# A fused four-layer graph network on one core: the GAT input loaded twice, the adjacency in four loads, P squared's copies moved, and new lists of steps

## The chip, the cores and the metric

The kernel runs on one core of a Trainium2 chip. Its time is the device time of one execution, in microseconds (us). Before the change the median of three runs was 1242.79 us (1241.85 to 1243.12).

## The reference

The input x has B = 16 batches of N = 512 nodes with D = 128 features, float32; adj is one 512 x 512 adjacency matrix for all batches. Four layers follow one another, each as x = x + layer(relu(layernorm(x))):

```python
# layer 0: eight Euler steps of a diffusion
h = h @ fc_in_w.T + fc_in_b
w_eff = w * clip(d, 0, 1) @ w.T
for _ in range(8):
    f = sigmoid(alpha)[:, None] * 0.5 * (adj @ h - h) + h @ w_eff - h + x0
    h = h + f / 8
# layer 1, GAT: attention over the graph
Wh = h @ W
e = leaky_relu(Wh @ a1 + (Wh @ a2).T); e = where(adj == 0, -inf, e)
out = softmax(e) @ Wh
# layer 2, edge: attention over 256 edges src -> dst, softmax by source node, then @ W_out.T
# layer 3: Chebyshev propagation, attention with 4 heads, feed-forward
L_norm = 2 * adj / (eigvalsh(adj)[-1] + 1e-8) - I
x1 = relu(layernorm((L_norm @ x) @ Wc + bc)) + x
x2 = layernorm(x1 + attention(x1 @ Wq, x1 @ Wk, x1 @ Wv, mask=adj > 0) @ Wo + bo)
out = layernorm(x2 + gelu(x2 @ W1 + b1) @ W2 + b2)
```

## The kernel before, in words

**Two programs behind one another.** `build_front` (line 563) computes what all batches share, the whole of layer 0, and, beside the last quarter of layer 0, layers 1 and 2 of the first batch and the start of layer 1 of the second. It ends near 453 us. `build_layers` (line 1824) does the rest as a pipeline over batches. Each engine runs its own program; they meet at semaphores. The engines are TensorE (PE), VectorE (DVE), ScalarE (ACT), GpSimd (POOL) and SyncE (SP), which issues the loads and stores, one behind another.

**Layer 0.** The eight Euler steps are written as polynomials: P = (sigmoid(alpha)/16) (adj - I), R = w_eff/8 + (7/8) I. The kernel loads adj in one transfer (line 683), transposes it on PE (`turn_adj`, line 1327) for S and the later Laplacian, transposes the 128 x 128 tiles of the weights (`turn_weights`), then those of P (`turn_p`, line 1341), keeps PT as a high and a low part of reduced precision (`keep_p`, `p_low`), and multiplies P by itself (`p_product`, line 1349). PE then makes R's powers (`r_product`), the products of R's powers with the fc weights and bias (`fc_products`, line 1369, and `bias_products`, line 1375). P squared is read out of PSUM by ACT, which writes its high part (P2T_hi, line 914), and by DVE (`p_squared`, line 1043), which writes a plain copy and the low part. In ACT's order the four copies of P2T_hi stand behind the ReLUs of batches 0 to 3; in DVE's, `r_powers(2)` stands behind `p_squared(0)` and `p_squared(1)`.

The 16 batches go through in four chunks of four. Batch by batch PE transposes the normalised input (`turn_x0`, line 1391) and applies P and P squared to it (`apply_p`, line 1398); the input z is split into a high part (ACT, `split_z`) and a low part (DVE, `split_z`, line 960); the products come out as U1 (kept by ACT) and U2 (kept by DVE, `keep_u2`, line 965). In chunk 0 each batch also makes a quarter of P cubed. Then per chunk three levels of four tiles follow (`right_products`, `p3_times`), which multiply with G, the polynomial table in R that DVE builds during chunk 0 (`polynomial`, line 1108).

**Asides and slots.** The largest eigenvalue of adj comes from nine squarings of a matrix S, hidden beside layer 0. Each batch and each tile is a *slot*, numbered through from 0; `aside(slot)` puts a piece of the squaring there, five slots to one squaring: the square sum (ACT), the norm's sum over partitions (PE, into PSUM), its reciprocal `nrm` (DVE, line 993), the scaled copies (ACT). In DVE's loop over batches (lines 1277 to 1296) the order is: split z of the batch after next, keep U2, cube and polynomial in chunk 0, and the aside last. On PE a transposition of the next batch's input (`turn_x0`) writes the same PSUM bank as the norm's sum, so it waits for `nrm`.

**Masks.** POOL makes two masks from adj in one instruction each: mask_gat (line 769), ahead of the first chunk's work, and mask_att (line 784), behind the square sums, in chunk 3.

**The pipeline.** Each stage of a batch (gat, edge, cheb, att, ffn) is cut into steps with a function each. `run` (line 1952) gives each engine its steps by lists written out by hand: FILL_ORDER (step:batch), then a loop whose iteration i runs each step of ORDER for batch i minus the stage's lag (gat 0, edge 1, cheb 2, att 3, ffn 4; each "+" behind a name is one batch more), then DRAIN_ORDER. The loop is rolled and runs iterations FILL to 15; FILL = 5 here, so 11 iterations. In the trace fill spans 453 to 579 us, the loop 579 to 1100, the drain the rest.

**GAT.** `load_x` (line 408) loads batch n's layer 0 output (256 KB) into xA once the last reader of xA for the batch before is done. `gat_stats` (line 456) reads xA, `gat_apply` (line 466) writes the normalised value to zA, `gat_turn` transposes zA on PE, ACT applies the ReLU (`gat_hT`, line 430), `gat_wh` is the first product. `gat_x2` (line 500), the stage's end, adds xA as the residual.

**Chebyshev, attention, ffn.** `cheb_prop` (line 2363 in the trace) multiplies by the Laplacian; its input is split by ACT (`cheb_hi`) and DVE (`cheb_lo`, line 2163). Q and K of each head go through memory and are loaded *stacked*, high and low part together (`stack0` to `stack3`). The attention runs 16 tiles: score (PE, line 2356), mask (DVE, line 2198), exponential (ACT, line 2100), turn (PE, line 2410), copy (ACT, line 2109), and at the end the product with V. In ffn the GELU's first call loads a table (ACT_TABLE_LOAD). An engine's copy from PSUM for several stages goes through one helper line, as L2085 on ACT.

## Time and profile before

| What | Value |
| --- | --- |
| Median of three runs | 1242.79 us (1241.85 to 1243.12) |
| The profiled execution | 1239.62 us, its span 1237.8 us |
| Granted TensorE clock, mean | 0.98 of full speed |
| PE busy | 1127.5 us (91%), 7537 instructions |
| DVE busy | 836.7 us (68%), 3039 instructions |
| ACT busy | 759.9 us (61%), 1625 instructions |
| POOL busy | 346.4 us (28%), 481 instructions |
| DMA | 83.59 MB moved, mean 68 GB/s |

The profile is of one execution of 1239.62 us; its times count from its own start, and the span ends 1.8 us short of that execution's time. A clock of 1.0 is 2.4 GHz and 0.5 is 1.2 GHz. An engine's busy time adds up its instructions; waits at semaphores, branches and the issue of DMAs are not in it. The columns of the rows are told at each group.

### The profile page before, as it was taken

The page shows a single profiled execution, that of the slowest core. Times are in us where ns is not written, and L with a number is a line of the kernel's source. Part 1 is how long each engine was busy: PE and PEld are TensorE (multiplying, and loading weights), DVE is VectorE, ACT ScalarE, POOL GpSimd, SP SyncE. Part 2 cuts the span into 40 slices and gives each one's busy share as a digit, 9 for nine tenths or more (in the row PEclk, how much of TensorE's full clock was granted, in tenths as well). Part 3 has the DMA queues.
Part 4 walks back from the last instruction along what each step waited for, and adds up shares of the span by engine and source line. Part 5 has one row for each costly group of instructions (what it writes and reads, how often), then busy time and mean ns, then how long its engine had stood idle before and what let it go on. Part 6 is the DMA issues. An engine that isn't in the chain of part 4 may idle for free. (4 is left out here: it accounts for less than half of the span.)

```text
span 1237.8 us, 23622 instructions
## 1 busy us (share of the span) xinstructions
PE 1127.5 (91%) x7537; PEld 894.1 (72%) x7537; DVE 836.7 (68%) x3039; ACT 759.9 (61%) x1625; POOL 346.4 (28%) x481
## 2 busy tenths in 40 slices
PE   7889999999999978899899999999999999999775
PEld 4568879889879865677767677677677677676554
DVE  5544213214336547888988988889889889888666
ACT  4314224333213235887978878878878878888763
POOL 3204006004042122242343333333423422422122
PEclk9899999999999989999999999999999999999898
DMA  5011020020010002334243242242242341342430
GB/s 126 17 33 28 26 73 5 27 76 2 26 52 1 27 26 67 88 86 105 58 119 88 65 119 76 72 123 62 82 120 61 90 119 51 102 109 68 109 91 26
DMA packets 123819, 83.59 MB, mean 68 GB/s; under 512 B 13296, under 2 KB 106864, under 8 KB 123760
## 3 DMA queue, kind: packets, MB, share of 16 engines
q1 hardware_dynamic: 123696, 82.82, 24.9%
q8 instruction: 34, 0.56, 0.2%
q14 instruction: 25, 0.20, 0.1%
q0 software_dynamic: 64, 0.00, 0.0%
HBM read 28.25 MB, written 20.97 MB: 40 GB/s over the span
## 5 line engine op out<-in xcount | busy, mean ns | idle before, releaser
L2100 ACT ACTIVATE att_Es<-att_Ts,att_small 128x512 f32<-128x512 f32 x256 | 184.8, 722 | 61.3 <-DVE att_small L2198 60.8
L2198 DVE CUSTOM_DVE_ANT_0 att_Ts<-bank,mask_att 128x512 f32<-128x512 f32 x256 | 174.2, 682 | 33.1 <-PE bank L2356 30.6
L2410 PE MATMUL bank<-ident,att_Es 128*128 128x128 f32 x1024 | 159.7, 279 | 20.1 <-ACT att_PTs L2109 18.8
L2410 PEld LDWEIGHTS bank<-ident,att_Es 128*128 128x128 f32 x1024 | 120.9, 142 | 62.4 <-ACT att_PTs L2109 35.6
L2109 ACT COPY att_PTs<-bank 128x512 f32<-128x512 f32 x248 | 143.4, 578 | 34.4 <-PE bank L2410 33.3
L2356 PE MATMUL bank<-K_parts,Q_parts 128*128 128x512 f32 x256 | 125.1, 498 | 2.7 <-DMA K_parts<-k_lo 1.8
L1908 POOL TENSOR_SCALAR n_rs<-n_mv 128x4 f32<-128x4 f32 x46 | 14.0, 304 | 289.0 <-DVE n_mv L1903 289.0
L424 POOL TENSOR_SCALAR gat_Vs<-gat_Ts,gat_small 128x512 f32<-128x512 f32 x64 | 57.7, 916 | 81.5 <-DVE gat_small L490 81.4
L974 DVE TENSOR_TENSOR P_row<-bank,l_bias 128x512 f32<-128x512 f32 x32 | 22.1, 691 | 84.0 <-PE bank L1426 65.9
L1416 PE MATMUL bank<-G,x0T 128*128 128x128 f32 x384 | 74.8, 276 | 0.7 <-DVE U2T L967 0.5
L1416 PE MATMUL bank<-G,U1T 128*128 128x128 f32 x384 | 74.3, 275 | 0.0
L1416 PE MATMUL bank<-G,U2T 128*128 128x128 f32 x384 | 74.2, 275 | 0.0
L722 POOL TENSOR_SCALAR l_rs<-l_mv 128x4 f32<-128x4 f32 x16 | 6.8, 425 | 230.9 <-DVE l_mv L958 230.6
L551 PE MATMUL bank<-gat_whs,gat_ETs 128*128 128x128 f32 x512 | 64.4, 282 | 2.1 <-PEq L141 2.0
L1416 PEld LDWEIGHTS bank<-G,x0T 128*128 128x128 f32 x384 | 60.5, 191 | 4.3 <-issue 1.7
L551 PEld LDWEIGHTS bank<-gat_whs,gat_ETs 128*128 128x128 f32 x512 | 61.2, 196 | 3.0 <-issue 2.5
L2356 PEld LDWEIGHTS bank<-K_parts,Q_parts 128*128 128x128 f32 x256 | 48.3, 194 | 20.6 <-issue 16.2
L1416 PEld LDWEIGHTS bank<-G,U2T 128*128 128x128 f32 x384 | 58.3, 192 | 0.0
L1416 PEld LDWEIGHTS bank<-G,U1T 128*128 128x128 f32 x384 | 58.3, 192 | 0.0
L442 ACT ACTIVATE gat_Ts<-gat_Vs,gat_small 128x512 f32<-128x512 f32 x64 | 46.3, 724 | 17.1 <-DVE gat_Vs L494 17.1
L2478 PE MATMUL bank<-att_PTs,v_in 128*32 128x512 f32 x480 | 54.3, 592 | 0.0
L1426 PE MATMUL bank<-Z_hi,P3T_hi 128*128 128x512 f32 x128 | 52.9, 414 | 0.0
(330 smaller groups left out, 2930.8 us busy)
## 6 DMA issues: line engine op xcount, KB each, us to landing
Q_parts<-q_hi SPq DMA_DIRECT2D x128, 64.0 KB, 2.0
Q_parts<-q_lo SPq DMA_DIRECT2D x128, 64.0 KB, 2.0
K_parts<-k_hi SPq DMA_DIRECT2D x128, 64.0 KB, 2.0
K_parts<-k_lo SPq DMA_DIRECT2D x128, 64.0 KB, 2.0
l_x<-in_x SPq DMA_DIRECT2D x16, 256.0 KB, 2.9
P2T<-in_x SPq DMA_DIRECT2D x16, 256.0 KB, 4.6
x_after_l<-P2T SPq DMA_DIRECT2D x16, 256.0 KB, 2.3
gat_xin<-x_after_l SPq DMA_DIRECT2D x16, 256.0 KB, 4.0
```

What stands on the lines that cost most here:

```text
L424: nc.gpsimd.tensor_scalar(g.V[:, t, :], g.T[:, t, :], 0.2, small[:, 5, t:t + 1], ALU.mult, ALU.add).then_inc(sem("gat_low"), 1)
L442: nc.scalar.activation(g.T[:, t, :], g.V[:, t, :], ACT.Exp, bias=small[:, 4, t:t + 1], accum_out=small[:, 6, t:t + 1]).then_inc(sem("gat_e ...
L551: mm = nc.tensor.matmul(a0[:, cols(t)], g.ET[:, s, cols(t)], WhA[:, s, 0:D], start=(s == 0), stop=(s == NT - 1))
L974: nc.vector.tensor_tensor(by_batch(zs[:, t, :]), by_batch(bank[t][:]), bias[:, BLOCKS - 1 - lev, t:t + 1, :].broadcast_to([P, CB, D]), ALU.add
L1416: mm = nc.tensor.matmul(bank[t][:, b * D:(b + 1) * D], UT[i][:, b, cols(t)], G[:, STEPS - k0 - i, :], start=(b == 0 and i == 0), stop=(lev ...
L1426: mm = nc.tensor.matmul(bank[t][:], left[:, s, cols(t)], right[:, s, :], start=False, stop=(s == NT - 1 and i == 2))
L2100: nc.scalar.activation(att_E[:, j % RING_E, :], att_T[:, j % RING_T, :], ACT.Exp, scale=-1.0, bias=att_small[:, 0, j:j + 1], accum_out=att ...
L2109: nc.scalar.copy(att_PT[:, h, :, cols(q)], c2[:].rearrange("p (s q) -> p s q", q=P)).then_inc(sem("att_pt"), 1)
L2198: nc.vector.tensor_tensor_reduce(att_T[:, j % RING_T, :], [c0, c1][j % 2][:], k.mask_att[:, tile_of(n, j)[1], :], -QK_SCALE, HUGE, ALU.add ...
L2356: return nc.tensor.matmul(dst, left, right, start=True, stop=True)
L2410: mm = nc.tensor.transpose(dst[:, cols(s)], att_E[:, i % RING_E, cols(s)], k.ident[:])
L2478: mm = nc.tensor.matmul(b0[r, :], vD[:, s, r], att_PT[:, h, s, :], start=(s == 0), stop=(s == NT - 1))
```

## The change

1. The GAT input is loaded twice: `load_z` fills zA for the statistics and the normalising, which is now done in place; `load_x` fills xA, read only by the residual addition at the stage's end. `load_z` waits for PE's transposes of the batch before, `load_x` for the last residual addition as before.
2. In the front, adj comes in four loads of 128 rows, each with its own semaphore (shared with the later loads of the residual). PE transposes the rows' tiles in the order in which they are loaded, then P (`turn_p`), then the weights. DVE makes P's rows as they come. The four semaphores stand for the one in POOL too.
3. ACT copies the high part of P squared (`square_hi`) right behind P's: two copies ahead of the first ReLU, two behind the second; the casts of S and the other ReLUs follow. DVE's order is p_squared(0), r_powers(0), the row sums of P, p_squared(1), r_powers(1), statistics(2), p_squared(2), statistics(3), r_powers(2), p_squared(3), then the splits of z.
4. In DVE's loop over batches the aside comes first from chunk 1 on, and in chunk 0 right behind U2 and the split of z, ahead of the cube and the polynomial; keeping U2 comes ahead of the split of z.
5. POOL makes mask_att in four instructions, and behind `edge_pick` instead of ahead of it.
6. ORDER, FILL_ORDER and DRAIN_ORDER are written anew. In ORDER six steps gain a "+": load_x3, ffn_final, store_out, stack0 and stack2, edge_store, so FILL becomes 6: the loop runs 10 iterations, and one more batch is written out in FILL_ORDER. On PE gat_turn moves from behind cheb_g to ahead of ffn_wo, gat_wh in between cheb_prop1 and cheb_g, and some turns, scores and ffn products change places. On DVE ffn_final+ and att_rv+ move to the top, the GAT statistics ahead of the masks. On ACT gat_hT moves up between att_exp1 and att_exp2, att_copy2 behind ffn_x2T, att_copy3 between the two GELUs.

```diff
@@ gat_stage
     def on_sync(sp):
+        def load_z(n):
+            wait_alone(sp, sem("gat_turned"), n, sem("waits_passed"))
+            sp.dma_start(zA[:], k.nodes1(k.x1_dram, n)).then_inc(sem("gat_zloaded"), 16)
         def load_x(n):
             wait_alone(sp, sem("gat_done"), n * NT, sem("waits_passed"))
...
         def gat_stats(n):
-            ready(dve, "gat_loaded", n, 16, 16)
+            ready(dve, "gat_zloaded", n, 16, 16)
             for t in range(NT):
-                nc.vector.bn_stats(g.stat[:, t, :], xA[:, t, :]).then_inc(sem("gat_stat"), 1)
+                nc.vector.bn_stats(g.stat[:, t, :], zA[:, t, :]).then_inc(sem("gat_stat"), 1)
...
         def gat_apply(n):
+            ready(dve, "gat_stat", n, NT, NT)
             ready(dve, "gat_rs", n)
             for t in range(NT):
-                nc.vector.tensor_scalar(zA[:, t, :], xA[:, t, :], ...
+                nc.vector.tensor_scalar(zA[:, t, :], zA[:, t, :], ...
...
         def gat_x2(n, t0):
             if t0 == 0:
+                ready(dve, "gat_loaded", n, 16, 16)
                 ready(dve, "gat_rinv", n)
@@ build_front, SP
-            load(adj[:], t_in["adj"].rearrange("(t p) m -> p t m", p=P), "adj_loaded")
+            for t in range(NT):
+                load(adj[:, t, :], t_in["adj"][t * P:(t + 1) * P, :], f"rows_loaded{t}")
@@ build_front, POOL
-            pool.wait_ge(sem("norm_part"), SQUARINGS)
-            nc.gpsimd.tensor_scalar(k.mask_att[:], adj[:], 0.0, MASKED / QK_SCALE, ALU.is_le, ALU.mult
-                                    ).then_inc(sem("masks"), 1)
             pool.wait_ge(sem("u_ready"), 2 * B)
             for t in range(NT):
                 nc.gpsimd.tensor_scalar(k.edge_pick[:, t, E:], edge_f[:, 1, :], node_col[:, t:t + 1], None,
                                         ALU.is_equal).then_inc(sem("pick"), 1)
+            pool.wait_ge(sem("norm_part"), SQUARINGS)
+            for t in range(NT):
+                nc.gpsimd.tensor_scalar(k.mask_att[:, t, :], adj[:, t, :], 0.0, MASKED / QK_SCALE, ALU.is_le, ALU.mult
+                                        ).then_inc(sem("masks"), 1)
@@ build_front, ACT
+            def square_hi(s):
+                act.wait_ge(sem("p_square"), s + 1)
+                nc.scalar.copy(P2T_hi[:, s, :], bank[4 + s][:]).then_inc(sem("P2T_hi"), 1)
+
+            square_hi(0)
+            square_hi(1)
             for b in range(2):
                 relu(b)
                 split_z(b)
+            square_hi(2)
+            square_hi(3)
             act.wait_ge(sem("asym"), NT)
             nc.scalar.copy(S[0][:], asym[:]).then_inc(sem("scaled"), 1)
             for b in range(2, CB):
                 relu(b)
-            for s in range(NT):
-                act.wait_ge(sem("p_square"), s + 1)
-                nc.scalar.copy(P2T_hi[:, s, :], bank[4 + s][:]).then_inc(sem("P2T_hi"), 1)
@@ build_front, DVE
+            p_squared(0)
+            r_powers(0)
             nc.vector.tensor_reduce(pone[:, 0, :], P_row[:], AX, ALU.add).then_inc(sem("p_one"), 1)
-            r_powers(0)
-            for b in range(2, CB):
-                statistics(b)
+            p_squared(1)
             r_powers(1)
-            for s in range(2):
-                p_squared(s)
+            statistics(2)
+            p_squared(2)
+            statistics(3)
             r_powers(2)
+            p_squared(3)
             for b in range(2):
                 split_z(b)
-            for s in range(2, NT):
-                p_squared(s)
...
                     b = ch * CB + j
+                    if ch:
+                        aside(slot)
+                    keep_u2(b)
                     if j < CB - 2:
                         split_z(b + 2)
-                    keep_u2(b)
                     if ch == 0:
+                        aside(slot)
                         p_cubed(j)
...
-                    aside(slot)
                     slot += 1
@@ build_front, PE
+            def turn_adj():
+                for t in range(NT):
+                    pe.wait_ge(sem(f"rows_loaded{t}"), 16)
+                    for s in range(NT):
                         mm = nc.tensor.transpose(bank[4 + s][:, cols(t)], adj[:, t, cols(s)], k.ident[:])
+                        if t == NT - 1:
+                            mm.then_inc(sem("adj_turned"), 1)
...
-            turn_adj("adj_turned", None)
+            turn_adj()
+            turn_p()
             turn_weights()
-            turn_p()
@@ ORDER
     "PE": """
-        att_score0 att_score1 att_turn15+ att_rows+ att_pv0+ att_pv1+ att_score2 att_turn0 att_score3 cheb_prop0
-        ffn_wo att_turn1 att_score4 cheb_prop1 cheb_g gat_turn att_turn2 att_score5 gat_wh ffn_turn att_turn3 gat_s2
-        ffn_up0 att_score6 ffn_up1 att_turn4 ffn_down0 att_score7 ffn_down1 att_turn5 att_score8 cheb_x1turn att_turn6
...
+        att_score0 att_score1 att_turn15+ att_rows+ att_pv0+ att_pv1+ att_score2 att_turn0 att_score3 gat_turn ffn_wo
+        cheb_prop0 att_turn1 att_score4 cheb_prop1 gat_wh cheb_g att_turn2 ffn_turn att_score5 gat_s2 ffn_up0
+        att_turn3 att_score6 ffn_up1 att_turn4 att_score7 ffn_down0 ffn_down1 att_turn5 att_score8 cheb_x1turn
...
     "DVE": """
-        cheb_stats cheb_aggr gat_x2a+ gat_x2b+ edge_stats att_mask0 edge_aggr att_mask1 cheb_lo gat_stats gat_aggr
-        att_mask2 att_scale att_mask3 gat_apply ffn_y2 n2_stats att_mask4 n2_aggr cheb_y n2_apply n1_stats att_mask5
...
+        cheb_stats ffn_final+ cheb_aggr gat_x2a+ gat_x2b+ att_rv+ gat_stats gat_aggr att_mask0 edge_stats edge_aggr
+        att_mask1 gat_apply cheb_lo att_scale att_mask2 att_mask3 ffn_y2 n2_stats n2_aggr att_mask4 n2_apply cheb_y
...
     "ACT": """
-        cheb_apply cheb_hi att_spread+ att_exp0 att_exp1 att_exp2 att_copy0 att_exp3 edge_apply cheb_xpT att_copy1
-        att_exp4 gat_hT att_copy2 edge_hi gat_wh_out0 gat_wh_out1 ffn_x2T att_exp5 att_copy3 ffn_gelu0 ffn_gelu1
-        att_exp6 att_copy4 att_exp7 att_copy5 cheb_x1T att_exp8 att_copy6 gat_exp0 edge_hg gat_exp1 edge_xz att_exp9
...
+        cheb_apply cheb_hi att_spread+ att_exp0 att_exp1 gat_hT att_exp2 att_copy0 att_exp3 edge_apply cheb_xpT
+        att_copy1 gat_wh_out0 att_exp4 edge_hi gat_wh_out1 ffn_x2T att_copy2 att_exp5 ffn_gelu0 att_copy3 ffn_gelu1
+        att_exp6 att_copy4 att_exp7 att_copy5 cheb_x1T att_exp8 att_copy6 gat_exp0 edge_hg gat_exp1 edge_xz
...
     "POOL": """
-        cheb_rstd edge_rstd ffn_res gat_rstd n2_rstd n1_rstd ffn_b2 edge_lo gat_low0 gat_low1 gat_low2 gat_low3
+        cheb_rstd gat_rstd edge_rstd ffn_res n2_rstd ffn_b2 edge_lo n1_rstd gat_low0 gat_low1 gat_low2 gat_low3
...
     "SP": """
-        load_xr load_x3 load_x stack1+ stack3+ store_v+ load_v cheb_res stack0 stack2 edge_store store_out
+        load_z load_x3+ stack0+ stack2+ store_out+ load_xr stack1+ load_x stack3+ edge_store+ store_v+ load_v cheb_res
...
@@ FILL_ORDER, its beginning
     "PE": """
-        gat_pv0:1 gat_pv1:1 cheb_prop0:0 cheb_prop1:0 cheb_g:0 edge_gather0:1 edge_gather1:1 gat_turn:2 edge_x:1
+        gat_pv0:1 gat_pv1:1 cheb_prop0:0 cheb_prop1:0 cheb_g:0 gat_turn:2 gat_wh:2 gat_s2:2 edge_gather0:1
...
     "DVE": """
-        cheb_stats:0 gat_rinv:1 cheb_aggr:0 gat_x2a:1 gat_x2b:1 edge_stats:1 edge_aggr:1 cheb_lo:0 gat_stats:2
+        cheb_stats:0 cheb_aggr:0 gat_rinv:1 gat_x2a:1 cheb_lo:0 gat_x2b:1 gat_stats:2 gat_aggr:2 edge_stats:1
...
```

## Rows read from the trace of the kernel before

**Rows 1.** Busy by stage: stretch, length, busy (count) of PE, PEld, DVE, ACT, POOL, clock, DMA.

```profile
14.25:44.04 29.79, 24.46 (x81) 12.93 (x81) 20.52 (x69) 12.14 (x24) 18.84 (x21) 0.89 0.17 31
450.00:484.89 34.89, 24.17 (x130) 19.05 (x130) 23.61 (x94) 12.89 (x29) 10.48 (x17) 0.90 0.14 40
484.89:628.22 143.33, 131.98 (x923) 101.87 (x923) 119.87 (x468) 116.00 (x264) 43.25 (x66) 0.99 0.32 85
628.22:1099.99 471.77, 441.04 (x3223) 338.69 (x3222) 419.76 (x1631) 395.81 (x880) 165.49 (x231) 1.00 0.33 89
1099.99:1237.80 137.81, 107.96 (x785) 75.51 (x783) 97.21 (x339) 91.06 (x195) 31.55 (x44) 0.92 0.31 82
```

**Rows 2.** Timeline (start, duration, engine, line, operation, tiles, shape, [idle before]): SP's load of adj.

```profile
1.24 0.50 SPq L674 DMA_DIRECT2D adj<-in_adj  x1
```

**Rows 3.** Timeline of PE: transposes of adj and P, first product with P.

```profile
6.81 3.67 PE L1332 MATMUL bank<-ident,adj 128*128 128x128 f32 x16 [6.81 <-DMA adj<-in_adj]
...
11.07 1.91 PE L1346 MATMUL bank<-ident,P_row 128*128 128x128 f32 x16
...
14.25 3.70 PE L1352 MATMUL bank<-PT,P_row 128*128 128x512 f32 x8 [1.26 <-DVE PT L1035]
```

**Rows 4.** Timeline, 33 to 44 us: the mask, P squared's copies, fc and bias products.

```profile
33.26 7.12 POOL L769 TENSOR_SCALAR mask_gat<-adj 128x2048 bf16<-128x2048 f32 x1
...
35.36 0.69 DVE L1045 COPY P2T<-bank 128x512 f32<-128x512 f32 x1 [9.00 <-ACT P2T_hi L914]
...
38.49 3.46 PE L1372 MATMUL bank<-Rp,raw_fcw 128*128 128x512 f32 x4 [5.04 <-DVE Rp L1067]
...
42.25 1.96 PE L1379 MATMUL bank<-Rp,fcb_b 128*128 128x512 f32 x4 [0.29 <-DVE pone L1273]
```

**Rows 5.** Timeline: G's operations, the transposes behind the reciprocal at slot 1 and later.

```profile
65.08 3.23 DVE L1114 SCALAR_TENSOR_TENSOR G<-Rp,G 128x128 f32<-128x128 f32 x15
...
68.45 0.81 PE L1395 MATMUL bank<-ident,l_x 128*128 128x128 f32 x4 [4.52 <-DVE nrm L993]
...
251.42 0.66 PE L1395 MATMUL bank<-ident,l_x 128*128 128x128 f32 x4 [0.74 <-DVE nrm L993]
```

**Rows 6.** Busy by stretch, columns as in rows 1: behind three waits.

```profile
68.45:76.00 7.55, 7.55 (x28) 6.20 (x29) 0.00 (x0) 1.84 (x3) 0.00 (x0) 0.77 0.14 37
164.26:171.84 7.58, 7.58 (x28) 6.27 (x29) 0.00 (x0) 1.84 (x3) 0.00 (x0) 0.77 0.12 35
362.37:366.79 4.42, 4.42 (x12) 3.49 (x13) 1.87 (x9) 0.00 (x0) 1.39 (x1) 0.62 0.01 2
```

**Rows 7.** Timeline of PE: the transposes behind the reciprocal at slot 17.

```profile
164.26 1.05 PE L1395 MATMUL bank<-ident,l_x 128*128 128x128 f32 x4 [2.05 <-DVE nrm L993]
```

**Rows 8.** Timeline: a split of z in chunk 0, then chunk 3 with the mask.

```profile
61.13 0.69 DVE L962 TENSOR_TENSOR z_split<-l_x,z_split 128x512 fp32r<-128x512 f32 x1 [1.85 <-ACT z_split L813]
...
356.66 7.10 POOL L784 TENSOR_SCALAR mask_att<-adj 128x2048 bf16<-128x2048 f32 x1
357.21 4.50 DVE L962 TENSOR_TENSOR z_split<-l_x,z_split 128x512 fp32r<-128x512 f32 x1 [6.24 <-ACT z_split L813]
...
362.37 0.79 PE L1407 MATMUL bank<-P2T_hi,z_split 128*128 128x512 f32 x1 [2.55 <-DVE U2T L967]
```

**Rows 9.** Waits, 628.22 to 1099.99 us: us in total, times, longest us.

```profile
DVE gat_stat L459 <- DMA gat_xin<-x_after_l: 13.0, 10, 1.7
...
PE bank L2501 <- ACT ffn_mT L2093: 11.0, 10, 1.1
...
PE bank L2352 <- ACT cheb_xTs L2085: 6.9, 10, 0.7
PE bank L2352 <- DVE att_oTs L2277: 6.1, 10, 1.1
```

**Rows 10.** Timeline of ACT: a table load ahead of GELU in the loop.

```profile
835.25 1.28 ACT L2093 ACT_TABLE_LOAD   x1
```

**Rows 11.** Timeline of PE: the first propagation, in the fill.

```profile
461.82 0.79 PE L2363 MATMUL bank<-lap_hi,h_hi 128*128 128x512 f32 x1 [3.19 <-DVE h_lo L2163]
```

310 lines of the change are left out of this document (165 added, 145 removed).

## The prediction

> **What bounds the kernel now.** I read the busy time by stage first [rows 1]; the columns to compare are the length of a stretch and the matmul engine's (PE's) busy time in it. From 628 to 1100 us, ten batches at 47.2 us, PE is busy 441.04 of 471.77 us, so it sets the pace and 3.07 us a batch are its waits. VectorE (DVE) follows with 419.76 us. So a gain must come out of PE's idle time or out of stretches where its clock was granted at half. Idle are 5.3 us between the first product with P and 44.04, 10.7 and 11.4 us while the pipeline fills, 30.7 us in the loop and 29.9 us at the end. Next I went through PE's timeline for each idle stretch and what ended it, and through the waits of the loop.
>
> **Start: adjacency in four loads, P turned ahead of the weights.** One load is issued at 1.24 us [rows 2] and ends PE's first wait at 6.81; 16 transposes take 3.67 us; P's own turning starts at 11.07 and the first product with P at 14.25, after 1.26 us of waiting for DVE's copy [rows 3]. With quarters the transposes of three are done by the time the fourth lands. It carries the same last byte, so I leave it at 6.8; its four transposes take 0.9 us (a quarter of 3.67), until 7.7 instead of 10.5. ScalarE (ACT) can then no longer copy between transposes: its four copies, some 0.55 us each, end at 10.0, and P's turning ends behind them, at 10.5 to 11.6 by the clock. DVE's last copy of P follows, so the first product starts near 12.3: **1.95 us saved**. Ends: 3 us if PE runs at full speed by then, 0.5 us if the three added issues of 0.50 us [rows 2] push the last landing. The weights' five transposes fall into PE's wait and cost nothing; without that cover they are 0.6 us.
>
> **P squared's copies.** PE stood 5.04 us until 38.49 because DVE's copy of the highest power of R is queued behind P squared's first halves, and these waited 9.00 us for ACT [rows 4], whose copies stood behind four batches' ReLUs. The two fc products then ran at half clock, 3.46 us against 1.96 us for the next pair of the same shape, and the bias products waited 0.29 us more. In the new lists each copy follows its product. Without a stall the stretch is: 19.2 us from the first product to 33.45 (38.49 less 5.04), then 1.96 and 1.96, together 23.1 of the present 29.79 us: **6.7 us saved**. I followed the other queues through it with the old durations: DVE has R's power at 28.7 (PE wants it at 31.5), ACT has the cast of S at 29.6 and the fourth ReLU at 33 (PE wants its result 12 us later), GpSimd (POOL) ends its sums for batch 3 at 31.2.
>
> **The norm's reciprocal ahead of other work.** At slot 1 PE has made the norm's sum and waits 4.52 us for its reciprocal, since DVE first runs 15 operations of G, 3.23 us [rows 5]. The same hand-over with nothing ahead costs 0.74 us (at 251.42). Moving the reciprocal first leaves 0.74: 3.8 us. The idle spell was followed by half clock: 7.55 us at a mean of 0.77 [rows 6] lose 1.7 us. **5.5 us saved.** At slot 17 it is 2.05 us [rows 7] with 7.58 us at 0.77: 1.3 and 1.7, **3.0 us saved**. What waits behind the reciprocal now is U2's copy and G: U2 is read one slot, some 6 us, later, and G is done near 80 of the present clock, ten us before its reader; that slack is their cover.
>
> **POOL's big mask.** In chunk 3 DVE's split of z took 4.50 us instead of 0.69 while POOL made the attention mask in one instruction of 7.10 us begun 0.55 us before it; U2 came late and PE waited 2.55 us [rows 8], then ran 4.42 us at 0.62 [rows 6], 1.7 us lost. The mask now stands behind the edge tables, in four pieces. **4.2 us saved.** It falls beside layer 0's additions of the last chunk, where DVE's subtractions have two SBUF inputs again; a piece may hold one by up to 1.8 us, but the first matmul that reads them comes 2 to 4 us later, so I count zero (ends 0 and 2). The Trainium skill's page "SBUF — State Buffer", section "Who interferes with whom", says that a VectorE instruction with two SBUF inputs and a GpSimd one that reads SBUF exclude each other for a whole instruction, whichever starts first. The trace agrees here (4.50 us against 0.69).
>
> Layer 0 with the start: 21.4 us.
>
> **The input loaded twice.** In the loop DVE waits 1.3 us a batch for that load [rows 9], since it may start only when the previous batch's last reader is done. The second buffer is free after PE's transposes, half a batch earlier. The wait goes, but DVE is not the bound; its worth is that normalising, transposing and the GAT's first product can come earlier, into PE's holes. The 16 added loads of 256 KB go onto SP's queue, at most 0.50 us of issue each [rows 2]. The first stands behind one wait that is long over, and the stacked Q and K of heads 1 and 3 move ahead of the other; the tightest, head 1's, keeps the margin of 0.7 us it has. They are hidden.
>
> **New lists in the loop.** PE waits there 1.10, 0.69 and 0.61 us a batch for GELU, the Chebyshev copy and the scaled output [rows 9]. The new list puts GAT's product between the second propagation and its reader, GAT's transposes ahead of the output product, and a score ahead of the down product. The first two waits so covered go (1.3 us). Against that the copy behind attention turn 3 now stands behind the first GELU and the 1.28 us table load [rows 10]: exponential 0.8, table 1.28, GELU 0.64, copy 0.5, together 3.2 us, against 2.4 us of PE work; turn 5 waits similarly for the table coming back. Walking one batch through the new lists with the old durations I get some 2.3 us of waits instead of 3.07: 0.75 us a batch, for the 11 batches from the third on **8.2 us**. Ends: 0 and all three waits, 2.4 us a batch.
>
> **Fill and drain.** The first propagation waited 3.19 us for DVE's low part [rows 11], ahead of which stood GAT's last additions and edge's statistics; all but the first pair of these additions now stand behind it, 2.4 us of work by my walk. With the half clock after the wait and shorter waits later I take **4 us** of the 22 idle (ends 0 and 8). At the end, **1.8 us** of 29.9 (ends minus 2 and 6).
>
> **Sum.** 21.4 + 8.2 + 4 + 1.8 = 35.4 us. The profiled execution took 1239.62 us; 1204.2 after. The median of the runs is 3.2 us above that execution, so 1207.4 us.
>
> **Rivals.**
> 1. *A new lock at the start.* POOL's other big mask now starts at 31.3 by my walk, DVE's second split of z at 30.75. If POOL is first, DVE stands as in [rows 8], some 4.4 us from POOL's start, until 35.7; the bias products then start at 36.6 instead of 33.2 and PE's clock halves after the wait: 5.1 us given back, 1212.5 us. For it: half a microsecond of margin in a walk whose steps are good to 0.3. Against: the mask took 7.12 us from 33.26 in the old kernel [rows 4] and nobody stood, since DVE's work came after its first 4.4 us. By the skill's rule on that page the outcome hangs on who starts first, which is this rival.
> 2. *The lists only move the waits.* ACT's table load and, at the top of the loop, POOL's residual addition beside DVE's low part (my walk puts them 0.2 us apart) take back what was won: loop and drain 0, fill 2. 1239.62 − 23.4 + 3.2 = 1219.4 us.
> 3. *Slower: GAT's early transposes hold ACT.* GAT's ReLU now stands ahead of the third exponential. If its input comes late, all exponentials wait. It decides from 0.5 us late on (that is the slack of the first copy behind it); at 3.5 us late each of 14 batches loses 3 us and gains 0.75: 31.5 us lost against 21.4 won, with nothing from fill and drain, 1252.9 us. Against: its load is issued some 20 us ahead.
> 4. *Quarters do not land earlier.* The last lands 1.5 us later than the whole did; then only 0.5 us of the first term stays, 1208.9 us. The skill's "DMA: Bandwidth & Descriptors", section "Bandwidth", asks for 1 MiB or more per DMA, which speaks for this rival; no row here shows a quarter of this load.
>
> **How the numbers follow.** Forecast 0.60, rival 1 0.17, rival 2 0.16, rival 3 0.03, rival 4 0.04. Low end: 1.5 instead of 0.75 us a batch, 8 us more, and 1 us of the first term: 1198. High end: rival 2, and half of rival 1's price with it: 1222. A measurement of this kernel can tell 0.2% (2.5 us) from no change. Only rival 3 is above: slower 0.03; 0.01 for a mixture near zero; faster 0.96.
>
> **What would show it.** Right: the first product with P near 12.3; P transposes of batch 0 near 35.5 us with no wait over 1 us before; 0.7 us at both reciprocals; no split of z over 0.7 us in chunk 3; the clock at full from 15 us to the end of layer 0; layer 0's last product some 21 us earlier; no DVE wait for GAT's input; a batch in the loop at 46.4 us, PE's waits at GELU and the copy behind turn 3. Wrong: a split of z of 3 to 5 us beside the first mask (rival 1); 47.2 us a batch (rival 2); ACT idle before GAT's ReLU by more than 1 us (rival 3); PE's last adjacency transposes after 9 us (rival 4).

## The result, and the profile after

The changed kernel took 1206.66 us in the median of four runs (1199.74 to 1207.36) where the kernel before took 1242.32 us (1241.63 to 1243.12): a ratio of 0.9697, 95% interval 0.9658 to 0.9736. Six more runs on another chip gave 1206.33 us (1200.88 to 1208.19) against 1246.19 us, ratio 0.9672 (0.9639 to 0.9705). The forecast was 1207.4 us, range 1198 to 1222.

The four runs spread over 8 us where the four of the kernel before lay within 1.5, but on the other chip eleven runs of the kernel before spread over 12 us (1240.31 to 1252.38) and six of the changed one over 7, so a wide spread did not come with the change. The profiled execution is one of the short ones, 1199.74 us with a span of 1197.9 us. A second profile, of an execution of 1205.45 us, is read beside it below. So the time fell by 40.0 us between the first two profiles (1237.84 to 1197.86) and by 34.2 us to the second. The sum of the prediction, 35.4 us, is to be held against both.

The busy time by stage answers to [rows 1]. Columns as there: stretch, its length, busy time and count of PE, PEld, DVE, ACT and POOL, granted clock, DMA share and GB/s. The cuts are at 12.3 and 37 us in the front, at layer 0's last product, at the first scores of batches 0, 3 and 13, and at the end.

```profile
12.30:37.00 24.70, 24.70 (x94) 14.35 (x93) 23.02 (x68) 12.39 (x25) 17.86 (x21) 1.00 0.31 58
421.08:460.57 39.49, 27.67 (x160) 20.08 (x159) 26.78 (x102) 17.65 (x41) 11.22 (x19) 1.00 0.21 57
460.57:600.97 140.40, 128.25 (x916) 101.24 (x915) 119.88 (x465) 112.94 (x260) 43.74 (x66) 0.99 0.34 90
600.97:1056.39 455.42, 433.59 (x3223) 338.62 (x3222) 416.43 (x1631) 393.07 (x880) 165.63 (x231) 1.00 0.36 97
1056.39:1197.86 141.47, 110.45 (x785) 75.80 (x783) 96.49 (x340) 90.50 (x195) 31.53 (x44) 0.91 0.31 83
```

In the front's stretch PE has no idle time left and its full clock in this execution. Ten batches of the loop take 455.42 us instead of 471.77, 45.5 us each; the same 3223 matmuls are busy for 433.59 us instead of 441.04. The end, with the same 785 matmuls, is longer: 141.47 against 137.81 us.

Where PE reached the same points, in the three profiles (start times of the first transposes, products or scores, from the timelines):

| PE's point | Before | After, 1st | After, 2nd | Saved, 1st | Forecast |
| --- | --- | --- | --- | --- | --- |
| first product with P | 14.25 | 11.85 | 12.05 | 2.40 | 1.95 |
| x0 transposes, batch 0 | 44.04 | 34.43 | 36.33 | + 7.21 | 6.7 |
| x0 transposes, batch 3 | 80.36 | 64.89 | 66.79 | + 5.86 | 5.5 |
| x0 transposes, batch 8 | 251.42 | 232.53 | 234.43 | + 3.42 | 3.0 |
| layer 0's last product | 444.43 | 421.08 | 426.19 | + 4.46 | 4.2 |
| first score, batch 2 | 579.44 | 553.61 | 560.23 | + 2.48 | 4 |
| first score, batch 13 | 1099.99 | 1056.39 | 1063.00 | + 17.77 | 8.2 |
| end of the span | 1237.84 | 1197.86 | 1203.66 | - 3.62 | 1.8 |

**Start.** DVE makes P's rows as the quarters land. Its timeline, and PE's:

```profile
4.24 0.49 DVE L1029 TENSOR_SCALAR P_row<-adj,sg 128x512 f32<-128x512 f32 x1 [0.43 <-DMA adj<-in_adj]
...
6.88 0.49 DVE L1029 TENSOR_SCALAR P_row<-adj,sg 128x512 f32<-128x512 f32 x1 [0.24 <-DMA adj<-in_adj]
...
8.60 1.98 PE L1365 MATMUL bank<-ident,P_row 128*128 128x128 f32 x16 [0.31 <-DVE P_row L1034]
```

The last quarter is there at 6.88 us, where the whole was at 6.81 [rows 3]. The loads share the same last byte, as assumed. The first quarter is there at 4.24.

**P squared and the reciprocals.** PE's timeline of the front has no wait over 0.3 us between 12 and 65 us:

```profile
27.43 3.63 PE L1406 MATMUL bank<-pone,PT 128*128 128x1 f32 x32
30.91 1.96 PE L1391 MATMUL bank<-Rp,raw_fcw 128*128 128x512 f32 x4
32.72 1.88 PE L1398 MATMUL bank<-Rp,fcb_b 128*128 128x512 f32 x4
...
54.57 0.66 PE L1414 MATMUL bank<-ident,l_x 128*128 128x128 f32 x4 [0.26 <-DVE nrm L1010]
```

The 5.04 us of [rows 4] are gone, and the 4.52 us of [rows 5] are 0.26. Rival 1 did not come: DVE's two splits ran from 29.43 and POOL's mask began at 31.37, 0.66 us behind their end. The mask held DVE all the same, but at a copy that PE does not wait for: the one at 33.52 took 5.04 us (the timelines of the two):

```profile
29.43 1.28 DVE L979 TENSOR_TENSOR z_split<-l_x,z_split 128x512 fp32r<-128x512 f32 x2
...
31.37 7.12 POOL L779 TENSOR_SCALAR mask_gat<-adj 128x2048 bf16<-128x2048 f32 x1
...
33.52 5.04 DVE L1098 COPY src_rows<-rowv 128x128 f32<-128x128 f32 x1
```

**The loop.** PE's waits over the ten batches (total us, times, longest) answer to [rows 9]:

```profile
PE bank L2452 <- ACT att_PTs L2151: 18.8, 20, 1.4
...
PE bank L352 <- DVE edge_small L290: 2.6, 10, 0.3
...
PE bank L2398 <- DMA K_parts<-k_lo: 0.2, 1, 0.2
```

The waits for GELU, for the Chebyshev copy and for the scaled output are gone. Those for the attention's copies have grown from two of 0.42 us together in a batch to 1.37 and 0.52 us, both behind the GELU. DVE's wait of 1.3 us for GAT's load is no longer listed.

### The profile page after: what moved, and what is told of

It reads as the page before. It is cut to its first block and busy times, and to the rows that moved or that the text cites. A ratio compares the mean times of both kernels' runs of the same rounds, so it can differ in the third digit from the quotient of the medians.

```text
span 1197.9 us, 23544 instructions
## 1 busy us (share of the span) xinstructions
PE 1111.4 (93%) x7537; PEld 887.8 (74%) x7537; DVE 833.2 (70%) x3039; ACT 754.3 (63%) x1625; POOL 347.7 (29%) x484
## 5 line engine op out<-in xcount | busy, mean ns | idle before, releaser
L2398 PE MATMUL bank<-K_parts,Q_parts 128*128 128x512 f32 x256 | 122.5, 488 | 4.0 <-DMA K_parts<-k_lo 4.0
L428 POOL TENSOR_SCALAR gat_Vs<-gat_Ts,gat_small 128x512 f32<-128x512 f32 x64 | 60.3, 955 | 66.3 <-DVE gat_small L495 66.3
L984 DVE COPY U2T<-bank 128x512 f32<-128x512 f32 x16 | 11.1, 691 | 63.8 <-PE bank L1426 63.8
```

Source lines behind the costliest of these rows:

```text
L428: nc.gpsimd.tensor_scalar(g.V[:, t, :], g.T[:, t, :], 0.2, small[:, 5, t:t + 1], ALU.mult, ALU.add).then_inc(sem("gat_low"), 1)
L2398: return nc.tensor.matmul(dst, left, right, start=True, stop=True)
```

## Experiments

Each ran with its own runs of the kernel before on the same chip. The medians are of five or six runs.

**The changed kernel again.** No edit.

> The changed kernel once more. Its runs so far lie in two groups, 1199.4 to 1199.7 us with a mean granted clock of 0.987 to 0.988, and 1206.1 to 1207.4 us with 0.980 to 0.984. Theory: the schedule is the same in both and the 7 us are further stretches at half clock behind waits of PE; a profile of the slower group then shows the same waits but a granted clock under 1.0 in windows where the first profile had 1.00, 7 us of delay in those windows alone. Rival: a wait of its own, a DMA that lands later or an engine pair that meets differently, with a clock that only follows; then a wait is longer by over 1 us ahead of each such window.

Measured: 1206.33 us. The profile is of an execution of 1205.45 us and is the table's column "After, 2nd". In its front, PE ran this (timeline, then busy time by stretch):

```profile
27.62 3.63 PE L1406 MATMUL bank<-pone,PT 128*128 128x1 f32 x32
31.11 3.18 PE L1391 MATMUL bank<-Rp,raw_fcw 128*128 128x512 f32 x4
34.08 2.41 PE L1398 MATMUL bank<-Rp,fcb_b 128*128 128x512 f32 x4
...
329.82 4.74 PE L1474 MATMUL bank<-vec,asym 128*128 128x1 f32 x32
334.42 1.09 PE L1414 MATMUL bank<-ident,l_x 128*128 128x128 f32 x4
```
```profile
27.60:34.10 6.50, 6.50 (x38) 4.69 (x37) 4.12 (x10) 4.94 (x9) 5.93 (x7) 0.82 0.00 0
...
329.80:337.00 7.20, 7.20 (x41) 6.82 (x40) 4.46 (x15) 1.20 (x2) 4.22 (x5) 0.66 0.42 106
```

No idle time stands ahead of either place. What stands there is 32 products with one column each; the products behind them are slower (3.18 us against 1.96), at a mean clock of 0.82 and 0.66. Against the first profile, the first place costs 1.7 us (another 0.2 us stood ahead of it, at the first product with P) and the second 3.2, together 4.9 of the 5.8 us between the two profiles. The theory that it is the clock holds for these, but not its words "behind waits": PE was busy.

**The front alone.** The changed front, with one load of GAT's input and the old lists.

```diff
-            ready(dve, "gat_zloaded", n, 16, 16)
+            ready(dve, "gat_loaded", n, 16, 16)
...
     "SP": """
-        load_z load_x3+ stack0+ stack2+ store_out+ load_xr stack1+ load_x stack3+ edge_store+ store_v+ load_v cheb_res
+        load_xr load_x3 load_x stack1+ stack3+ store_v+ load_v cheb_res stack0 stack2 edge_store store_out
```

> The changed front with the GAT input loaded once and the old lists of steps. Theory (the parts add up): layer 0's last product 23.3 us earlier than before, as in the changed kernel, fill, loop and drain as before, 47.2 us a batch: 1242.3 less 23.3 = 1219 us. Rival: part of the front's gain is lost again where the old fill waits, at least 5 us: 1224 us or more.

Measured: 1220.83 us (1213.47 to 1228.42) against 1246.19. In the medians 25.4 us come from the front and 14.5 us from the rest, so the parts add up within the noise. The spread is 15 us, with a clock of 0.989 in the shortest run and 0.976 in the longest. The profile is of the longest, 1228.42 us: there layer 0's last product is at 428.59 us, only 15.8 us earlier than before instead of 23.3, with half clock behind both sets of one-column products; a batch takes 47.3 us.

**Two loads with the old lists.** SP has `load_z` where `load_x` stood and `load_x` behind stack3+.

```diff
-        load_xr load_x3 load_x stack1+ stack3+ store_v+ ...
+        load_xr load_x3 load_z stack1+ stack3+ load_x store_v+ ...
```

> The changed front and the input loaded twice, but the old lists (the first load where the only one stood, the second behind head 3's stack). Theory: the second buffer is worth nothing by itself, since DVE's wait of 1.3 us a batch for that load is not PE's; 47.2 us a batch, 1219 us, within 2 us of the kernel with the front alone. Rival: half of the loop's 1.7 us a batch comes from it: 46.4 us a batch, 1210 us.

Measured: 1220.09 us (1217.14 to 1222.87), 0.7 us from the front alone. The second buffer is worth nothing by itself. More than that, DVE still waits (waits from 654.71 to 1080.02 us, some nine batches):

```profile
DVE gat_stat L463 <- DMA gat_z<-x_after_l: 12.2, 9, 1.9
```

The load stands behind others in SP's list and is issued no sooner: in batch 8 it is issued 1.75 us after the batch's first score, in the kernel before 1.81 us after it. With the new lists it is issued 24.0 us after the first score of the batch before.

**One load with the new lists.** As the changed kernel, but the single load stands behind load_x3+ and ahead of stack0+.

```diff
-        load_z load_x3+ stack0+ stack2+ store_out+ load_xr stack1+ load_x stack3+ ...
+        load_x3+ load_x stack0+ stack2+ store_out+ load_xr stack1+ stack3+ ...
```

> The changed front and the new lists, but the input loaded once, behind the last reader of the batch before. Theory: the new lists need the second buffer; DVE has the GAT statistics right behind that last reader and stands there for the landing, some 3 to 4 us a batch; its slack in a batch of 45.5 us is 3.9 us and PE waits behind it: 47 to 49 us a batch, 1217 to 1245 us. Rival: DVE's slack takes all of it, 45.5 us a batch and 1200 to 1207 us.

Measured: 1335.62 us (1331.59 to 1338.88), 55.8 us a batch, worse than either theory. The timelines of SP, DVE and PE, and PE's wait over 9 batches:

```profile
910.57 1.09 DVE L507 SCALAR_TENSOR_TENSOR x<-bank,gat_small,gat_xin 128x128 f32<-128x128 f32 x4
...
911.92 0.38 SPq L410 DMA_DIRECT2D gat_xin<-x_after_l  x1
912.66 1.18 SPq L2038 DMA_DIRECT2D Q_parts<-q_hi  x2
...
919.14 1.22 PE L2391 MATMUL bank<-K_parts,Q_parts 128*128 128x512 f32 x2 [7.54 <-DMA K_parts<-k_lo]
```
```profile
PE bank L2391 <- DMA K_parts<-k_lo: 70.9, 15, 7.6
```

The load may be issued only when DVE's residual addition is done (911.66), and SP holds the stacks of Q and K behind it. PE then waits 7.5 us for them and runs the stretch at a clock of 0.93. So what the new lists need of the second buffer is shown for this place of the load only: that GAT does not hold SP. Another place for the single load was not tried.

**The reciprocal's old place.**

```diff
-                    if ch:
-                        aside(slot)
-                    keep_u2(b)
                     if j < CB - 2:
                         split_z(b + 2)
+                    keep_u2(b)
                     if ch == 0:
-                        aside(slot)
                         p_cubed(j)
...
+                    aside(slot)
```

The edit moves two things back: the reciprocal, and keeping U2 behind the split of z.

> The changed kernel with DVE's loop over batches as before (split of z, U2, cube and polynomial, reciprocal last). Theory: the reciprocal stands behind G again; PE waits 4.5 us at slot 1 and 2.0 us at slot 17, with a half clock behind each; the x0 transposes of batch 3 come 5.8 us later against the changed kernel's and those of batch 8 another 3.4: 9.2 us in all, 1215.5 us. Rival: with P squared's stall gone the hand-over at slot 1 has changed, and the wait is under 2 us: 1210 us or less.

Measured: 1216.39 us (1214.16 to 1219.28), 10 us more than the changed kernel. PE's timeline:

```profile
62.90 1.12 PE L1412 MATMUL bank<-ident,l_x 128*128 128x128 f32 x4 [4.52 <-DVE nrm L1010]
...
159.68 0.66 PE L1412 MATMUL bank<-ident,l_x 128*128 128x128 f32 x4 [2.05 <-DVE nrm L1010]
```

Both waits are back to a hundredth of those of [rows 5, 7]. From batch 0 to batch 8 the transposes are 246.86 - 38.47 = 208.39 us apart, in the changed kernel 232.53 - 34.43 = 198.10: 10.3 us. The waits are for `nrm`, so this term is settled: it is worth what was forecast (8.5 us) and some more.

**The attention mask in its old place.**

```diff
+            nc.gpsimd.tensor_scalar(k.mask_att[:], adj[:], ...)
             pool.wait_ge(sem("u_ready"), 2 * B)
...
-            for t in range(NT):
-                nc.gpsimd.tensor_scalar(k.mask_att[:, t, :], adj[:, t, :], ...)
```

> The changed kernel with the attention mask in one instruction of 7.1 us in its old place, ahead of the edge tables. Theory: a split of z takes 4.5 us again, PE waits for U2 and its clock halves: the x0 transposes of batch 15 come 4.4 us later against those of batch 13; 1210.7 us. Rival: since keeping U2 now stands ahead of the split of z, the long split has no reader for a batch and a half: it still takes 4.5 us, but PE doesn't wait, and the time is that of the changed kernel, 1206.3 us within 1.5.

Measured: 1205.41 us (1201.41 to 1208.49), nothing lost. The rival's number is right, but its reason wasn't put to the test: in the profile (1205.41 us) the split did not stand at all. The timelines of POOL and DVE:

```profile
338.69 7.10 POOL L794 TENSOR_SCALAR mask_att<-adj 128x2048 bf16<-128x2048 f32 x1
...
343.09 0.69 DVE L978 TENSOR_TENSOR z_split<-l_x,z_split 128x512 fp32r<-128x512 f32 x1
```

The split came 4.4 us after the mask's start, and by then the mask no longer holds it (in [rows 8] the split ended 5.05 us after the mask's start). In this execution PE had run the second set of one-column products and batch 13 at half clock, 3.2 us lost; no profile shows the old place in an execution without that loss. The shortest run, 1201.41 us, lies within 2 us of the changed kernel's shortest (1199.74), so a loss of 4 us isn't seen there either.

**Three parts undone.** P squared's copies and DVE's order around them, the reciprocal, the mask.

```diff
-            square_hi(0)
-            square_hi(1)
...
             for b in range(2, CB):
                 relu(b)
+            for s in range(NT):
+                square_hi(s)
...
-            p_squared(0)
+            nc.vector.tensor_reduce(pone[:, 0, :], P_row[:], AX, ALU.add).then_inc(sem("p_one"), 1)
             r_powers(0)
...
+            for s in range(2):
+                p_squared(s)
             r_powers(2)
...
```

The other two edits are those above.

> The changed kernel with three parts undone together: P squared's copies and DVE's order around them, the reciprocal's place, and the attention mask in one instruction in its old place. Their places in the trace keep them apart. Theory for P squared: PE waits 5 us ahead of the fc products and runs them at half clock, the x0 transposes of batch 0 come 6 to 8 us later than in the changed kernel's first profile (34.43). Theory for the mask: it takes both undone to bring the wait back, since either U2 stands ahead of the split of z or the mask is out of its way; the split takes over 3 us, PE waits 2 us or more for U2, and the transposes of batch 15 come 4 us later against those of batch 14. Sum 7.5 + 9.2 + 4.4 = 21 us, 1227 us. Rival for the mask: its start against the split is chance of the clock; with it undone the split takes 0.7 us and PE does not wait: 1223 us.

Measured: 1222.2 us (1220.91 to 1226.56). The timelines of PE, then POOL and DVE:

```profile
36.17 3.78 PE L1386 MATMUL bank<-Rp,raw_fcw 128*128 128x512 f32 x4 [5.06 <-DVE Rp L1081]
```
```profile
356.53 7.10 POOL L794 TENSOR_SCALAR mask_att<-adj 128x2048 bf16<-128x2048 f32 x1
...
360.33 1.25 DVE L976 TENSOR_TENSOR z_split<-l_x,z_split 128x512 fp32r<-128x512 f32 x1 [8.73 <-ACT z_split L823]
```

P squared's stall is back, 5.06 us (5.04 in [rows 4]), and batch 0's transposes come 8.5 us later. The mask's is not: the split came 3.80 us after the mask's start and took 1.25 us, and PE did not wait. Here PE had run the one-column products and batch 13 at half clock, 3.2 us lost, so that DVE's split met the mask 3.25 us later than in [rows 8]. So the old place costs 4.2 us in an execution in which the two collide, and nothing in one in which the clock has fallen before.

**The one-column products in halves.** Both sets of 32 are cut in two, with full products between.

```diff
             r_product(1)
+            p_ones(0)
             p_product(PT, 3, 7, "p_square")
             r_product(2)
-            p_ones()
+            p_ones(1)
...
                     for which in range(2):
                         apply_p(b, which)
+                        if which == 0 and b == B - CB:
+                            top_eigenvalue(0)
```

> The changed kernel with its two sets of 32 one-column matmul records (the row sums of P squared's vector, 3.6 us, and the eigenvalue's matrix-vector product, 3.6 to 4.7 us) cut in halves, with full products between. Theory: in the slower group of executions the clock fell behind these stretches although PE was never idle (1.9 us lost near 33 us, 3.2 us near 334 us); in halves they no longer bring it down: clock 1.0 from 12 to 420 us in the profile, the slower group gone, mean clock 0.987 or more in most runs, median 1200 to 1202 us. Rival: the clock falls by chance, not by what PE ran: the two groups stay, median 1206 us.

Measured: 1206.27 us (1204.67 to 1209.63), mean clocks 0.984 to 0.989. In the profile the clock stayed at 1.0 behind both sets, and yet the time is the same. The timelines of POOL, DVE and PE:

```profile
31.88 7.12 POOL L779 TENSOR_SCALAR mask_gat<-adj 128x2048 bf16<-128x2048 f32 x1
...
32.16 5.38 DVE L979 TENSOR_TENSOR z_split<-l_x,z_split 128x512 fp32r<-128x512 f32 x2
...
37.76 3.20 PE L1398 MATMUL bank<-Rp,fcb_b 128*128 128x512 f32 x4 [3.94 <-DVE pone L1290]
```

This is the prediction's rival 1, set off by 1.8 us of products ahead of P squared's last: the mask starts 0.28 us ahead of the splits, these take 5.38 us instead of 1.28, and PE waits and then runs at half clock. From its first product with P to batch 0's transposes PE needs 5.4 us more than in the changed kernel's first profile; the rival was priced at 5.1. From batch 12 to batch 15, PE needs 21.92 us.

**The same, cut between the fc products.**

```diff
-            p_ones()
-            fc_products()
+            p_ones(0)
+            fc_product(0)
+            p_ones(1)
+            fc_product(1)
```

> As thin_split, but the first set is cut between the fc products (half, first fc product, half, second fc product), so that P squared's last product and DVE's queue keep their times. Theory: DVE's splits of z end before POOL's mask begins, 0.7 us each; clock 1.0 from 12 to 420 us; the x0 transposes of batch 0 at 34.4 to 35 us and layer 0's last product at 421 to 422 us in the profile; median 1200 to 1203 us. Rival: the clock falls whether or not the one-column products are together; layer 0's last product at 424 us or later, median 1206 us.

Measured: 1201.97 us against 1244.54 (ratio 0.9675), with all six runs from 1201.37 to 1204.09. The median is where theory put it, but not its trace: with only one fc product (1 us) between the halves, the clock still fell (the fc products at 29.03 and 32.00 us took 1.10 and 2.05, the bias products 3.62), and layer 0's last product is at 424.52 us. Cut by batch 12's products, the second set again left the clock at 1.0.

**The copy ahead of the GELU.**

```diff
     "ACT": """
-        ... att_exp5 ffn_gelu0 att_copy3 ffn_gelu1
+        ... att_exp5 att_copy3 ffn_gelu0 ffn_gelu1
```

> The changed kernel with the copy behind attention turn 3 ahead of the first GELU in the loop's list of ACT. Theory: the 1.37 us a batch that PE waits for that copy are the table load and the first GELU ahead of it; with the copy first PE has that turn at once, and waits some 0.6 us for the GELU instead, ahead of the down product: 0.5 to 0.8 us a batch less, 45.0 us a batch or less, 5 to 8 us in all, 1200 us. Rival: ACT's chain (table, two GELUs, table back) is the bound in this stretch, so the wait only moves behind the GELU and to the exponential: 45.5 us a batch, 1206 us.

Measured: 1205.22 us (1200.45 to 1212.34), 45.75 us a batch. PE's waits over ten batches:

```profile
PE bank L2543 <- ACT ffn_mT L2135: 14.9, 10, 1.5
PE bank L2452 <- ACT att_PTs L2151: 5.5, 10, 0.5
```

The rival is right. 1.49 us at the GELU's reader replace 1.37 at the copy's. That ACT's run of table load, two GELUs and table load back sets this stretch, whatever stands first, fits; it was not isolated.

**The old drain lists.** PE's, ACT's and POOL's lists of before; DVE's and SP's of before with the steps put in that the new loop leaves over.

```diff
     "DVE": """
-        att_rv:12 cheb_stats:14 cheb_aggr:14 gat_x2a:15 gat_x2b:15 ffn_final:11 edge_stats:15 att_mask0:13
-        att_mask1:13 edge_aggr:15 cheb_lo:14 att_scale:12 ...
+        att_rv:12 cheb_stats:14 cheb_aggr:14 gat_x2a:15 gat_x2b:15 ffn_final:11 edge_stats:15 edge_aggr:15
+        att_mask0:13 cheb_lo:14 att_mask1:13 att_scale:12 ...
```

> The changed kernel with the drain lists of before (the few steps that the new loop leaves over put at their head). From score 0 of batch 13 to the end the changed kernel takes 141.5 us in one profile and 140.7 in another, the kernel before 137.85. Theory: the new drain lists are the longer ones; with the old ones 138 us, and the time falls by 3 us to 1203.3 us. Rival: the time comes with the work that the loop now leaves over and with clock spells, not from the lists: 141 us, 1206.3 us.

Measured: 1202.54 us (1196.18 to 1205.25). Its drain took 136.71 us:

```profile
1057.58:1194.29 136.71, 105.50 (x785) 73.88 (x783) 96.75 (x340) 90.63 (x195) 31.47 (x44) 0.95 0.32 86
```

**All of it.** The old drain lists, the halves as in the first of the two experiments, and POOL's first mask held until both splits of z are done.

```diff
                 if ch == 0:
+                    pool.wait_ge(sem("z_lo"), 2)
                     nc.gpsimd.tensor_scalar(k.mask_gat[:], adj[:], ...)
```

> The changed kernel with three edits: the old drain lists (old_drain), the one-column products in halves as in thin_split, and POOL's first mask held until both first splits of z are done, so that these do not stand behind it. Theory: the splits take 0.7 us each, no wait of 3.9 us ahead of the bias products; clock 1.0 from 12 to 420 us; x0 transposes of batch 0 at 35 to 36 us, layer 0's last product at 422 to 423 us, drain 137 to 138 us; median 1196 to 1200 us and all runs within 4 us, faster than the changed kernel by 6 to 10 us. Rival: the half clock in the front comes in any case, and held back the mask meets a later DVE instruction: layer 0's last product at 424 us or later and 1202 us or more.

Measured: 1200.14 us, all five runs from 1199.25 to 1201.74; ratio to the kernel before 0.9654 (0.9630 to 0.9678). Busy time from 12 us to layer 0's last product, and of the drain:

```profile
12.00:421.14 409.14, 404.90 (x2425) 346.04 (x2425) 168.33 (x487) 134.46 (x240) 94.09 (x116) 1.00 0.12 35
1057.97:1197.68 139.71, 108.69 (x785) 77.13 (x783) 96.74 (x340) 90.57 (x195) 31.41 (x44) 0.91 0.31 84
```

Every point of the front is within 0.1 us of the changed kernel's short execution, and none of the five runs is in its longer group. The drain took 139.71 us this time. The median is 6 us below the changed kernel's, the low end of the 6 to 10 expected; but it comes from another chip, on which the kernel before was 3 us faster too (1243.31 against 1246.19), and the intervals of the ratios overlap. A gain over the changed kernel is likely, not shown.

## Why the prediction was right, and where it was not

**The front: right by its own steps.** Four of the five terms have their size: 2.40, 7.2, 5.9 and 3.4 us for 1.95, 6.7, 5.5 and 3.0. The stall at P squared and both reciprocal waits came back when undone. The two reciprocal terms are larger since 0.26 us of wait is left at each, not the 0.74 that the prediction took from a later slot. At the start "until 7.7" was 8.29 for the transposes; P's turning began 0.31 us behind them, where DVE's rows were ready.

**The mask: a term read from one execution.** The 4.2 us match the first profile (4.46). The step that failed is taking the coincidence in [rows 8] for a property of the old order. Where POOL's start lies against DVE's depends on how fast PE ran before, and in two profiles with the old place the split missed the mask. What the change is worth there is not a fixed number. Whether keeping U2 ahead of the split would by itself have covered a collision stays open, since none came in either.

**Two loads.** "Its worth is that GAT's work can come earlier" is borne out by its absence: without the new lists it brought 0.7 us. That DVE's wait goes was the list's doing.

**The loop: the waits right, the sum too small.** "Some 2.3 us of waits instead of 3.07" measured 2.18, and the wait behind turn 3, put at 0.8, measured 1.37. The step that failed is "0.75 us a batch": it takes PE's busy time as fixed, and that fell by 0.74 us a batch with the same instructions. The idle time in a row begins at the modelled end of the last product. In [rows 9]'s kernel the last propagation product before a wait counts 0.39-0.40 us of busy time, while the same product with another right behind it gives way after 0.23; the eight products behind the wait take 1.16 us instead of 1.06. PE's timeline in one batch of the kernel before:

```profile
640.19 0.40 PE L2363 MATMUL bank<-lap_hi,h_lo 128*128 128x512 f32 x1
641.27 1.16 PE L2352 MATMUL bank<-w_Wc,cheb_xTs 128*128 128x128 f32 x8 [0.69 <-ACT cheb_xTs L2085]
```

and in one of the changed kernel:

```profile
612.54 0.39 PE L2405 MATMUL bank<-lap_hi,h_lo 128*128 128x512 f32 x1
612.77 1.05 PE L532 MATMUL bank<-w_W1ga,gat_hTs 128*128 128x130 f32 x8
```

So each long wait costs 0.16 + 0.10, some 0.26 us more than its row says. Of the waits of a batch four are gone on balance (seven of 0.07 us and more before, three now), three of them long; 0.74 us is close to three times 0.26. The first part is well measured: the products of the Laplacian's high with h's low part, two of which stood ahead of a wait in each batch, are busy for 1.25 us a batch before and 0.93 now. The second is less clean: GAT's first product too took 1.16 us in the kernel before (at 643.55), behind a gap of only 0.01 us. The account fits but was not isolated. The Trainium skill's page "TensorE: Matmul & The Clock Gate", section "Single matmul latency", has a constant of 166 ns beyond the columns in the latency of a single bf16 matmul, at full clock; the 0.16 us of the rows agree. The whole makes 1.64 us a batch instead of 0.75, and 17.8 us for 11 batches instead of 8.2.

**The fill: the named gain came, the rest did not.** The low part is 2.2 us earlier against GAT's product ahead of it (435.52 - 429.82 = 5.70 us after it, 461.11 - 453.19 = 7.92 before), near the 2.4 of the walk. DVE and PE:

```profile
435.52 0.69 DVE L2205 TENSOR_TENSOR h_lo<-cheb_hs,h_hi 128x512 fp32r<-128x512 f32 x1 [1.13 <-ACT h_hi L2131]
...
436.26 0.50 PE L2405 MATMUL bank<-lap_hi,h_hi 128*128 128x512 f32 x1 [2.63 <-DVE h_lo L2205]
```

PE's wait there is still 2.63 us of 3.19, since its product ahead ran at full clock and ended 1.6 us sooner. The step that failed is "shorter waits later": from layer 0's last product to batch 2's first score PE is idle for 21.4 us where it was idle for 19.0. One wait for a head's stacked K alone is 3.0 us long (0.9 before). The term came to 2.5 us instead of 4 only because PE's busy time fell by 5.0 us there, with 8 instructions fewer in the stretch and a mean clock of 0.99 instead of 0.96.

**The drain: the sign was wrong.** 1.8 us were to be won, 3.6 were lost. With the new lists it took 141.5, 140.7, 139.4, 139.6, 140.2, 139.7, 140.0, 140.6 and 141.6 us in nine profiles, with the old ones 137.9, 140.1, 137.6, 136.7 and 139.7: 140.4 against 138.4 in the mean, with spreads of 2 and 3 us. The new lists are longer there, by about 2 us, and the clock scatters too: at a granted clock of 0.95 the drain took 136.7 us with the old lists, 139.7 and 140.0 with the new ones. Which of the steps does it stays open, and so does the rest of the 5.4 us by which the term was off: the 1.8 us to be won were worked out in no row.

**The median by luck in part.** Of the first profile's 40 us, the loop gave 9.6 more and the front 2 more than forecast, fill and drain 7 less (1.5 and 5.4). The median then lies 7 us above that profile by the clock, where the sum added 3.2. In the median the two errors cancel: 1206.66 for 1207.4.

## What to carry to other kernels

Follow each moved step through every queue with old durations: that gave the front to half a microsecond. Add something, here about a quarter of a microsecond, to each long PE wait that goes, since its row does not show what PE loses around it. Before counting a coincidence of two engines as won, look how far their starts lie apart in a second profile; and where two profiles of one kernel drift apart without a wait, look at the granted clock there and at what PE ran just before.

## What the runs showed of the hardware

**The clock fell though PE was busy.** In ten profiles of the changed front the 32 one-column products of the eigenvalue ran in one piece. PE went from batch 12 to batch 15 in 21.9 us in four of them, 23.5 in one and 25.1 in five; in these six it ran at half clock behind those products, with no idle time ahead of it. Cut in halves with 512-column products between, it took 21.9 us in all three profiles. Behind the 32 products of the front, also in one piece and without a wait, the clock fell in five of nine profiles; with 4.4 us of 512-column products between the halves it stayed at 1.0 in both, and with one fc product of 1 us between them it fell in the one that tried. So few profiles do not prove it. The spread of the times speaks for it only in part: with both sets cut, six runs lay within 2.7 us and five within 2.5 on chips where the kernel before spread over 9.8 and 7.2, but five lay within 5.0 where the kernel before spread over 4.1 (thin_split).

**A mask on POOL holds a split on DVE for about 4.4 us, and a copy until the mask ends.** The mask takes 7.1 us. With its start 0.28 us ahead of them the two splits of z took 5.38 us, at 0.55 us ahead one took 4.50, at 3.80 us 1.25, at 4.4 us 0.69. The held ones ended 5.05 to 5.07 us after the mask's start (the first of the two at 5.07), so less the 0.69 us of a split they were held until about 4.4 us, an estimate from these rows. DVE's copy `src_rows<-rowv` (128x128, both sides in SBUF) fared otherwise: begun 2.15 us after the mask's start it took 5.04 us, begun 1.10 us after it (the last experiment) 6.10 us, and both times it ended 7.2 us after the mask's start, just behind the mask's end; with no mask beside it, it took 0.22 us (in the run with three parts undone). The Trainium skill's page "SBUF — State Buffer", section "Who interferes with whom", has the exclusion last a whole instruction. The copy agrees, the split does not, and for it the measurement decides; so the prediction's "the trace agrees" is right that the two exclude each other and not that it lasts the whole mask. In the changed kernel this cost PE nothing: no engine waited for that copy.
